# Layer 2's product on four batches at once, with two levels of seven products

## The reference

```python
# x [8, 512, 2048] f32; eight batches, each with an adapter of its own
x = x + einsum('bsi,boi->bso', x, W0[itok_B_3_7])            # layer 1: weight by batch, 2048 x 2048
x = x + einsum('bti,oi->bto', x, W) + b \
      + 2.0 * einsum('btr,bro->bto', einsum('bti,bir->btr', x, A[itok_B_0_23]), B[itok_B_0_23])   # layer 2, rank 16
```

## Time and profile before

| | us |
|---|---|
| median of 3 runs (2774.22 to 2776.67) | 2774.69 |
| the profiled execution | 2774.51 |
| its span, first to last instruction | 2772.9 |
| PE busy | 2707.6 (98%), 11904 matmuls |
| DVE busy | 1281.4 (46%) |
| ACT busy | 605.0 (22%) |
| POOL busy | 393.8 (14%) |
| data moved by DMA | 644.76 MB, mean 233 GB/s |

### The profile page before, as it was taken

One profiled execution on the slowest core, in us unless ns is written; L12 is line 12 of the kernel. 1 busy time (PEld: TensorE's weight loads), 2 busy tenths in 40 slices (PEclk: granted clock), 3 DMA queues, 4 the chain that ended last, 5 costly groups with the idle time before them and its releaser, 6 DMA issues.

```text
span 2772.9 us, 29633 instructions
## 1 busy us (share of the span) xinstructions
PE 2707.6 (98%) x11904; PEld 2236.8 (81%) x11904; DVE 1281.4 (46%) x1656; ACT 605.0 (22%) x785; POOL 393.8 (14%) x738
## 2 busy tenths in 40 slices
PE   7999999999999999999997799999999999999998
PEld 6888888888888888888886588888888888888886
DVE  4454454454544545445442544455343644455442
ACT  3232242332322323323220111010101111011100
POOL 2111111111111111111113002210121101210010
PEclk9999999999999999999999899999999999999999
DMA  7565555566655656555549558895788758895674
GB/s 259 205 221 182 197 209 203 207 216 204 213 201 200 207 201 220 187 204 208 181 144 370 195 203 287 288 365 198 251 286 338 270 205 287 278 376 196 225 241 171
DMA packets 140829, 644.76 MB, mean 233 GB/s; under 512 B 19604, under 2 KB 19604, under 8 KB 104852
## 3 DMA queue, kind: packets, MB, share of 16 engines
q1 hardware_dynamic: 69556, 370.19, 38.2%
q0 software_dynamic: 71136, 272.68, 27.3%
HBM read 506.47 MB, written 136.31 MB: 232 GB/s over the span
## 4 chain that ended last, share of the span: by engine, by line
PE 93%; DVE 2%; DMA 2%; issue 1%; POOL 1%; ACT 0%; SPq 0%; DVEq 0%; POOLq 0%; ACTq 0%
PE bank L628 17%; PE bank L630 16%; PE bank L629 16%; PE bank L654 14%; PE bank L657 14%; PE bank L655 14%; DMA hs<-h_mix 1%; DVE bank L542 1%; PE bank L613 1%; PE bank L614 1%; PE bank L668 1%; POOL c_sum L267 1%; DVE xc L551 0%; DMA w_raw<-w0T 0%; PE bank L675 0%
## 5 line engine op out<-in xcount | busy, mean ns | idle before, releaser
L628 PE MATMUL bank<-x_hi,w_hi 128*128 128x512 f32 x2048 | 797.7, 390 | 16.6 <-DVE x_lo L454 16.6
L630 PE MATMUL bank<-x_hi,w_lo 128*128 128x512 f32 x2048 | 797.2, 389 | 0.0
L629 PE MATMUL bank<-x_lo,w_hi 128*128 128x512 f32 x2048 | 797.2, 389 | 0.0
L654 PE MATMUL bank<-xc,wl 128*128 128x512 f32 x1792 | 700.3, 391 | 40.1 <-DVE xc L551 23.3
L655 PE MATMUL bank<-xc,wl 128*128 128x512 f32 x1792 | 698.6, 390 | 0.0
L657 PE MATMUL bank<-xc,wl 128*128 128x512 f32 x1792 | 698.4, 390 | 0.0
L628 PEld LDWEIGHTS bank<-x_hi,w_hi 128*128 128x128 f32 x2048 | 384.8, 188 | 97.5 <-issue 16.3
L336 ACT ACTIVATE w_hi<-w_raw 128x1024 fp32r<-128x1024 f32 x256 | 257.5, 1053 | 935.9 <-PE bank L630 925.3
L630 PEld LDWEIGHTS bank<-x_hi,w_lo 128*128 128x128 f32 x2048 | 384.7, 188 | 80.0
L629 PEld LDWEIGHTS bank<-x_lo,w_hi 128*128 128x128 f32 x2048 | 384.8, 188 | 79.8
L654 PEld LDWEIGHTS bank<-xc,wl 128*128 128x128 f32 x1792 | 337.3, 188 | 115.1 <-DVE c_sum L572 17.3
(11 more groups left out here) (54 smaller groups left out, 1364.3 us busy)
## 6 DMA issues: line engine op xcount, KB each, us to landing
wl<-w1s SPq DMA_DIRECT2D x224, 1024.0 KB, 5.5
w_raw<-w0T SPq DMA_DIRECT2D x256, 512.0 KB, 5.8
w1s<-q_out POOLq DMA_DIRECT2D x56, 1024.0 KB, 6.2
x1s<-x_raw POOLq DMA_DIRECT2D x128, 256.0 KB, 2.3
c_sum<-x1s POOLq DMA_DIRECT2D x128, 256.0 KB, 5.8
yT<-c_sum POOLq DMA_DIRECT2D x128, 256.0 KB, 5.3
x_raw<-xT POOLq DMA_DIRECT2D x62, 512.0 KB, 4.4
q_raw<-w1T POOLq DMA_DIRECT2D x32, 512.0 KB, 9.3
```

The lines of the kernel that those rows point to most:

```text
L628: pe.matmul(sums[s][:], w_hi[s][:, k, :], x_hi[:, k, :], start=(k == 0), stop=False)
L629: pe.matmul(sums[s][:], w_hi[s][:, k, :], x_lo[:, k, :], start=False, stop=False)
L630: mm = pe.matmul(sums[s][:], w_lo[s][:, k, :], x_hi[:, k, :], start=False, stop=(k == KT - 1))
L654: pe.matmul(bank, w[:, 0, k, :], x[:, 0, :], start=(k == 0), stop=False)
```

## The change

Layer 2 now takes four batches as one product (2 groups in place of 4 pairs). The outer level has seven products over quarters of the features (8 tiles) by two batches; each of those is again made with seven inner products over 4 tiles by one batch. So there are 2 x 49 inner products, each of 4 output tiles of 4 k-blocks, 48 matmuls. The inner level's sums of results are partly made in PSUM: an inner product with `BEGIN` False goes on adding to the banks that the one before left (`start=False`). DVE then adds each bank into one or two `c_sum` tiles (`INTO`; one for the first two outer products, two for the other five).

The outer level's five sums of x1 (`xss`) are made by transfers in layer 1: besides the store to `x1s`, a tile is written to `xss` where the sum begins, and added to it by a DMA with `accum_op=ALU.add` afterwards. For a subtraction ACT first makes the negative (`x1_neg`, 64 times). Over a group this is 5 beginnings and 5 additions of 16 tiles each.

The weight's sums are now made in 28 units of 4 tiles of layer 1 each, seven pieces of 512 KB per unit, from one quarter (outer products 4 and 6) or two quarters (the other five) of 1 MB per unit. The low-rank term is no longer a part of layer 2's products: in layer 1, tiles 4 to 11 of the next batch, PE makes two low-rank tiles per tile (L750), DVE adds x1 and bias (`xr`), and POOL stores `cis`, from which `c_sum` is filled. The last batch's 16 follow in layer 2, in inner products 4, 5, 11 and 12.

The diff, cut to its core:

```diff
+INTO = [((3, 1),), ((0, 1),), ((0, 1), (3, 1)), ((2, 1), (3, -1)), ((1, 1), (3, 1)), ((0, -1), (1, 1)),
+        ((0, -1), (2, -1))]
+BEGINS = [(S1, S4, S6), (S3,), (S7,), ()]
+ADDS = [(), (S6,), (), (S1, S7)]
+SUBTRACTS = [(), (), (S4,), (S3,)]
+IN_X = [True, False, True, False, True, True, False]
+BEGIN = [True, True, False, False, False, False, True]
+BANK_BEFORE = [2, 2, 2, 2, 2, 1, 3]
+HAS_SUM = [False, True, True, False, True, True, False]
-    WL = 3
+    WL = 5
...
+            def load_xr(b, o):
+                i = b * NT + o
+                if i >= XR:
+                    pool.wait_ge(ci_stored[i % XR], i // XR * 16)
+                pool.dma_start(xr[i % XR][:], x1s[b, o]).then_inc(xr_loaded[i % XR], 16)
...
                     pool.wait_ge(x1_sum, n + 1)
                     pool.dma_start(x1s[b, t], x1_raw[s][:]).then_inc(x1_stored[s], 16)
+                    for i in BEGINS[quad]:
+                        pool.dma_start(xss[b // 4, i, b % 2, t % HALF], x1_raw[s][:]).then_inc(x1_stored[s], 16)
+                    for i in ADDS[quad]:
+                        pool.dma_start(xss[b // 4, i, b % 2, t % HALF], x1_raw[s][:],
+                                       accum_op=ALU.add).then_inc(x1_stored[s], 16)
+                    for i in SUBTRACTS[quad]:
+                        negatives += 1
+                        pool.wait_ge(x1_neg_done, negatives)
+                        pool.dma_start(xss[b // 4, i, b % 2, t % HALF], x1_neg[s][:],
+                                       accum_op=ALU.add).then_inc(x1_stored[s], 16)
                     if b < NB - 1 and t % KX == KX - 1:
                         load_x(b + 1, t // KX)
...
+            for quad in (3, 0):
+                for i in (0, 3, 1, 2):
+                    load_c(0, quad, i)
+            load_b(NB - 1, 0)
+            for o in range(XR):
+                load_xr(NB - 1, o)
...
+            act.wait_ge(x1_sum, TILES)
+            for s in range(1, SEQ):
+                for h in range(SPLITS):
+                    xc_hi(s, h)
+                if s == 1:
+                    h_hi(NB - 1)
+                if s == 2:
+                    b_hi(NB - 1, 0)
...
+                for m in range(Q):
+                    dve.wait_ge(acc_done, s * Q + m + 1)
+                    for quad, sign in INTO[o]:
+                        tile = c_sum[quad][:, i, m]
+                        if sign > 0:
+                            op = dve.tensor_tensor(tile, bank[m][:], tile, ALU.add)
+                        else:
+                            op = dve.tensor_tensor(tile, tile, bank[m][:], ALU.subtract)
+                    op.then_inc(acc_free, 1)
+                    if late:
+                        add_lora(NB - 1, first_tile + m, bank_y[m])
+                    if s > 0 and m in (1, 2):
+                        xc_lo(s + 1, m - 1)
+                    if m == Q - 1:
+                        add_terms(s + 2)
+                    if m == Q - 1 and s in (1, INNER + 1):
+                        b_lo(NB - 1, s // INNER)
```

More of the change, by code:

```diff
@@ L88, in build @@
             b_mix = sb1("b_mix", [P, HALF * P], F32R)
+            xr = [sb1(f"xr{i}", [P, TOK]) for i in range(XR)]
         sums = banks[0:2]
@@ L95, in sb2 @@
                 return second.enter_context(nc.sbuf_tensor(name, shape, dt))
[L97 to L107, removed]
+            wl = [sb2(f"wl{i}", [P, 2, Q, P], F32R) for i in range(WL)]
+            xq = [sb2("xq0", [P, Q, TOK])]
+            xc = [sb2(f"xc{i}", [P, 2, Q, TOK], F32R) for i in range(2)]
+            xq.append(sb2("xq1", [P, Q, TOK]))
+            xq3 = sb2("xq3", [P, Q, TOK])
+            xq.append(sb2("xq2", [P, Q, TOK]))
+            xq.append(xq3)
+            c3 = sb2("c3", [P, 4, Q, TOK])
+            c0 = sb2("c0", [P, 4, Q, TOK])
+            c2 = sb2("c2", [P, 4, Q, TOK])
+            c1 = sb2("c1", [P, 4, Q, TOK])
+            c_sum = [c0, c1, c2, c3]
+        bank_y, bank_x = banks[0:4], banks[4:8]
         ids_loaded = sem("ids_loaded")
@@ L326, in _ @@
[L326 to L328 removed]
+                    if b > 0 and t == LORA_FROM - 1:
+                        for o in range(2):
+                            load_xr(b - 1, o)
+                    for o in lora_tiles(b, t):
+                        if o + 2 < NT:
+                            load_xr(b - 1, o + 2)
+                    for o in lora_tiles(b, t):
+                        store_ci(b - 1, o)
@@ L330, in _ @@
+            for quad in range(4):
+                for i in range(4):
+                    pool.wait_ge(y_stored[quad][i], (1 + Q) * 16)
         @block.scalar
@@ new lines, in _ @@
+                    if b > 0 and t in (2, 7):
+                        b_lo(b - 1, t // 7)
+                    for i, o in enumerate(lora_tiles(b, t)):
+                        add_lora(b - 1, o, banks[3 + i])
+                    if n < UNITS * 4:
+                        split_q(n)
+                    if n == TILES - 4:
+                        for h in range(SPLITS):
+                            xc_lo(0, h)
+            add_terms(1)
+            for h in range(SPLITS):
+                xc_lo(1, h)
@@ L615, in add_h, with low_rank @@
                 mm.then_inc(h_done if t == NT - 1 else h_part, 1)
+            def low_rank(b, o, bank):
+                pe.wait_ge(b_ready, 2 * b + o // HALF + 1)
+                pe.matmul(bank[:], b_mix[:, o % HALF * P:(o % HALF + 1) * P], h_mix[:], start=True,
+                          stop=True).then_inc(lora_done, 1)
             for b in range(NB):
```

640 lines of the change are left out of this document (321 added, 319 removed).

## The result

The changed kernel takes 2792.19 us (median of 4, 2790.53 to 2796.53). The kernel before takes 2775.22 on the same chip (2774.22 to 2776.67). The ratio is 1.0064, 95% interval 1.0048 to 1.008: slower by 0.6%. The forecast was 2680, 112 us too low. In the table, each row's "loss" is its span less its matmuls at 0.2268 us, split into PE's idle time and what the busy time is above the matmuls' worth.

A forecast was written before the change was run, and what follows sets the result against it. It took PE's matmul count, plus what starves PE, as the bound. Its terms summed as 2772.9 - 152.4 - 43.4 + 10 + 8 + 5 + 18 + 60 = 2678.1 us of span, so 2680 us, eight in ten within 2612 to 2800.

The forecast's parts named there:

- Part 1: Layer 2's matmuls on PE: 4704 in place of 5376, 672 fewer at 0.2268 us each, -152.4 us.
- Part 3: Inside layer 2: DVE's 10.2 us of work hides behind PE's 10.9 us product, so no cost.
- The rival of DVE's chain: Layer 2: ACT and DVE waits make 40 products lose 2 us each, 2760 us in all; chance 0.10.
- Part 4: Last x piece at seven batch boundaries: lands 2.55 us later each time, +18 us (9 to 35).
- The upper end of 35: Last x piece at batch boundaries: the cost in us if three 256 KB additions' worth is ahead of it.
- Part 5: Layer 1's transfers, tiles 4 to 11 of batches 1 to 6: DMA engines full, additions at two stores, +60 us (0 to 134).
- The sign it named: Layer 1, tiles 4 to 11 of batches 1 to 6: a DMA share of 1.0, with PE waits from software-queue transfers.
- Part 2: Passage between layers and layer 2's holes: -43.4 us from old pauses, then new waits of +10, +8 and +5.
- The hole at inner product 3: Start of layer 2: the last batch's low-rank weight lands some 37 us after the last tile, +10 us (0 to 15).
- The two at `xr`: Layer 2, between inner products 4 and 5, and 11 and 12: `xr` stored and reloaded, 5 and 3 us (0 to 16).
- the group boundary: Layer 2, between the groups: 1 MB of `xq` queued behind 4 MB of other transfers, +5 us (0 to 10).
- The DMA engines keep up: Rival for layer 1: its transfers add no time and the rest stands, 2620 us; chance 0.23.

The follow-up runs named there:

- Experiment 7: The kernel before with only the 160 writes and 160 additions to `xss` added, layer 2 as it was and the sums unread: 2853.13 us, ratio 1.028.
- Experiment 2: The changed kernel with the x piece loaded ahead of the writes and additions to `xss` in POOL's list: 2750.34 us, 0.9913 of the kernel before.
- experiment 3: The changed kernel with a third slot for weight pieces and each unit's pieces split one tile later: 2746.32 us, 0.9899 of the kernel before.
- experiment 1: The changed kernel with the 160 additions to `xss` written as plain stores, sums left out: 2736.53 us, 0.9866 of the kernel before.
- experiment 5: The changed kernel with the edits of experiment 2 and experiment 3, plus earlier low-rank loads and hidden-state split for layer 2: 2680.21 us.
- experiment 6: experiment 5 with the 160 additions written as plain stores, sums of x1 left out: 2638.94 us, 0.9509 of the kernel before.
- experiment 10: experiment 5 with output stores one inner product later and the last x piece loaded in halves, both issued earlier: 2667.57 us, 0.9604 of the kernel before.
- experiment 8: experiment 5 with `xr` loads ahead of the `xss` writes and additions, and half the last low-rank weight loaded two inner products later: 2711.62 us.

## Why the prediction was wrong

The forecast's terms make a loss of 130.7 us, and 247.5 were measured; the 117 between them come from four places.

**Part 1, right.** 11232 matmuls, and in windows of layer 2 without holes 884 in 200 us, 0.2262 each.

**Part 3, right.** PE is busy 200.00 of 200 us there, DVE for 158.48, 79%. The rival of DVE's chain is out.

**Part 4, the step that failed: +53.** It took one write and one addition ahead of the last x piece at all seven boundaries, counted 1.35 us for their issue and one addition of 1.2 us in the engines, 18 us in seven, and took DVE's sum to be on time. Measured: 71.3. The issue's delay was right (1.34 at the first boundary). Three things were not.
- The list was that of the first batch. At three boundaries three additions stand there.
- The price of what is ahead was too low. Experiment 7 has it alone, with DVE's sum on time: holes of 5.8 us behind one write and one addition and of 10.1 behind three additions, 53.6 in all, where the forecast had 2.55 each.
- DVE's late sum had no term here. Experiment 2 has it alone, with nothing ahead of the piece: 30.6 us.

Together they make 71.3 and not 84, and the piece lands sooner after a late issue: at the first boundary 7.8 us behind it and 9.9 in experiment 7, at the third 11.9 and 13.7. The upper end of 35 was too low for the same three. Part 5 named DVE's delay, "some 4 us late, which the slot ahead covers", and put it in the wrong place: at a batch's end no slot covers it.

**Part 5, its place wrong, its size near by luck: -12.** It had 60 us in tiles 4 to 11 of batches 1 to 6, 104.4 us for each eight tiles in place of 94.4. The sign it named came, a DMA share of 0.98 to 1.02 in all six. But two of the six stretches have no pause at all, the others up to 3.4 us, and they last 94.3 to 100.4 us, 24 in all above the matmuls' time. Two of them:

```profile
469.12:569.37 100.25, 96.97 (x418) 79.01 (x416) 56.01 (x69) 29.70 (x41) 51.57 (x87) 0.98 1.02 346
910.17:1004.46 94.29, 94.29 (x417) 78.08 (x416) 54.53 (x70) 31.62 (x43) 49.08 (x90) 1.00 1.00 376
```

The 48 us that are set against the 60 here are other waits: about 18 at the first x piece and 30.2 at the low-rank products, and experiment 3 removes most of them by a slot and the order of splits, at the same bytes. That 48 is near 60 is chance. The price of an addition, two stores, was good: 2.2 by experiment 1. (In the Trainium skill, Collectives: The Full Stack, The bandwidth ceiling, the two source reads of an add make a ReduceScatter 1.93 times slower than an AllGather. No run here is a collective; the 2.2 of an accumulating transfer is in line with it and somewhat above.) That additions cost engine time shows as 56 us in experiment 1 and 41 in experiment 6, so the term wasn't empty; before the orders are mended most of it acts through the boundaries.

**Part 2, the passage and layer 2's holes: +19.** Forecast 10 + 8 + 5 = 23, measured about 42. Windows of the passage, then ACT's timeline there, with the wait for `b_raw`:

```profile
1669.00:1684.00 15.00, 4.47 (x18) 3.34 (x17) 4.20 (x7) 0.00 (x0) 7.51 (x15) 0.72 1.04 385
1703.00:1716.00 13.00, 5.12 (x19) 3.93 (x18) 5.88 (x7) 2.95 (x3) 0.00 (x0) 0.75 0.72 243
```
```profile
1686.06 2.01 ACT L514 ACTIVATE xc<-xq 128x1024 fp32r<-128x1024 f32 x2 [18.91 <-DVE xq L650]
1709.00 1.06 ACT L478 ACTIVATE b_mix<-b_raw 128x1024 fp32r<-128x1024 f32 x1 [20.94 <-DMA b_raw<-lora_b]
```

The hole at inner product 3 came with ACT's wait for `b_raw` in it and at 8.0 for 10, but that is luck in part: the weight was ready to split 49 us after the last tile and not 37, and the hole at inner product 1 had already taken 10.7 of that. The two at `xr` took 9.5 and 7.5 for 5 and 3, the group boundary 6.7 for 5. Missed was a hole of 10.7 us at inner product 1: DVE's split of the hidden state stood behind its first additions into `c`, whose loads land 16 to 36 us after their issue (median 22.3). In experiment 5, which sets it ahead of them, PE has no wait for it, and 6.0 are left at `xc`.

**The clock, in no term: some +51.** PE's busy time is 58.9 us above its matmuls' worth, 7.8 before. The profile shows it after the holes: in the boundary's 14 us the granted clock is 0.62, and after the hole at inner product 3 matmuls start 0.43 us apart for 5 us, then 0.23 again:

```profile
1714.67 0.43 PE bank L800
...
1720.11 0.23 PE bank L802
```

In experiments with smaller holes the excess falls, 33 us (2580.6 busy) in experiment 5 and 14 us (2561.6) in experiment 6. So here a microsecond of hole costs 0.3 to 0.4 more (51 us for the 123 of idle time added here, 19 for 59 in experiment 7). The rows for it stood in the forecast, 0.62 and 0.64 in the earlier trace rows. It was priced where a hole went (the 38.6 of Part 2) and left out, without a reason, where one came: the second step that failed.

53 - 12 + 19 + 51 = 111 of 117; the other 6 are small gaps, which I didn't assign.

**The rivals.** "The DMA engines keep up" (2620) is out, by the 41 and 56 us. "Slow additions, slower than before" gave 2880 from four stores for each: the sign was right, the mechanism not, since an addition is 2.2 stores and the heavy tiles keep PE nearly fed. The true result needed a rival that was not there: a piece that PE wants at once, behind additions in one queue. Experiments 5 and 10 show that some 3.4% and more can be had, once that piece and the splits are moved. That experiment 5 lands on the forecast's own 2680 is chance: its holes are not the forecast's.

## What to carry to other kernels

When new transfers are put into a queue, price first the one transfer that an engine waits for with no slack: all that is issued ahead of it counts with at least its full engine time, whatever the mean share of the engines says (0.80 in experiment 7, and 78 us lost), and read the list at every boundary, not at the first alone. Ask too whether the engine that triggers the transfer comes to it on time (30.6 us in experiment 2). Add the slower clock after a new hole on TensorE, 0.3 to 0.4 us for each microsecond here. And an order adds no bytes: moving loads and splits and adding one slot was worth 125 us here, more than the adding itself (41 to 56).

## What was not expected of the hardware

- An accumulating DMA from SBUF to DRAM moved 256 KB in 128 packets where a store takes 64 (10240 more for 160), and took 2.2 times a store's engine time. While little else ran, the engines were full at half their rate: in the changed kernel 215 GB/s at a share of 1.13, against 425 at 1.02 in the earlier trace rows.

```profile
626.50:629.50 3.00, 1.77 (x4) 1.49 (x5) 3.00 (x3) 3.00 (x4) 0.37 (x1) 0.68 1.13 215
```

- A wait on POOL for a store that it has just issued holds everything behind it: experiment 8 was 31 us slower, with 252.2 us of such waits for 142.0.
- With a share of 1.00 over 1200 us (experiment 10), PE was still busy for 97.5% of them.
